# Regrouping the columns of a merged weight: 392 + 392 + a rest into 512 + 512 + a rest

## The reference, cut to what matters

```python
H = x @ W.T
xa = x @ A[adapter].T                       # rank 16
y = H + scal[adapter] * (xa @ Bm[adapter].T)
result = y @ base_w.T + base_b
logits = y @ router_w.T + router_b          # 8 experts
gate = top2(softmax(logits))                # normalised, spread over 8
mid = (y @ lora_A) * gate                   # 8 x 16 columns
x = x + result + 2.0 * (mid @ lora_B)
```

## Time and profile before

| | |
|---|---|
| median of 3 runs | 2394.57 us (2393.4 to 2395.55) |
| span of the profiled execution, first to last instruction | 2381.5 us |
| median less that span | 13.1 us |
| TensorE matmul, busy | 2354.5 us, 99% of the span |
| mean granted TensorE clock | 0.996 of full speed |
| weight stage, first matmul to last | 1781.8 to 1897.1 us |
| last stage, first matmul to end of the span | 1897.3 to 2381.5 us |

### The profile page before, as it was taken

One profiled execution on the slowest core, in us unless ns is written; L12 is line 12 of the kernel. 1 busy time (PEld: TensorE's weight loads), 2 busy tenths in 40 slices (PEclk: granted clock), 3 DMA queues, 4 the chain that ended last, 5 costly groups with the idle time before them and its releaser, 6 DMA issues.

```text
span 2381.5 us, 35318 instructions
## 1 busy us (share of the span) xinstructions
PE 2354.5 (99%) x12762; PEld 2074.8 (87%) x12762; DVE 1664.0 (70%) x2874; ACT 1369.5 (58%) x2256; POOL 1414.4 (59%) x1032
## 2 busy tenths in 40 slices
PE   8989999999999999999999999999999999999999
PEld 5778888888888888888888888888889999999999
DVE  6888888888888878888888788888862244444443
ACT  5767777777767767777777777777761211111110
POOL 4027888787778777777777777777710122222222
PEclk9999999999999999999999999999999999999999
DMA  9998999999998999989989989899876354444441
GB/s 343 385 328 283 285 291 272 288 282 287 278 298 279 284 282 280 281 277 287 282 274 288 284 276 282 275 290 280 274 196 132 87 140 130 130 130 130 128 121 60
DMA packets 250352, 582.33 MB, mean 245 GB/s; under 512 B 82745, under 2 KB 106682, under 8 KB 250178
## 3 DMA queue, kind: packets, MB, share of 16 engines
q1 hardware_dynamic: 183202, 401.18, 51.5%
q0 software_dynamic: 55584, 160.02, 26.0%
q10 hardware_dynamic: 11392, 18.88, 2.2%
HBM read 456.51 MB, written 123.45 MB: 244 GB/s over the span
## 4 chain that ended last, share of the span: by engine, by line
PE 93%; POOL 2%; DMA 2%; issue 1%; DVE 1%; ACT 0%; ACTq 0%; SPq 0%; DVEq 0%; POOLq 0%
PE ps L808 25%; PE ps L821 21%; PE ps L920 17%; PE ps L807 12%; PE ps L878 5%; PE ps L804 4%; PE ps L677 2%; PE ps L913 2%; PE ps L805 2%; POOL Xg L573 1%; PE ps L687 1%; PE ps L893 1%; DMA Xg<-yd,idx 1%; PE ps L700 1%; PE ps L699 0%
## 5 line engine op out<-in xcount | busy, mean ns | idle before, releaser
L808 PE MATMUL ps<-XX,HR 128*128 128x512 f32 x2688 | 961.0, 397 | 0.0
L573 POOL DMA_INDIRECT Xg<-yd,idx x504 | 663.4, 1316 | 160.5 <-issue 152.7
L807 PE MATMUL ps<-XX,LR 128*128 128x256 f32 x2688 | 751.2, 279 | 0.1
L1540 DVE TENSOR_TENSOR LR<-raw,HR 128x1536 fp32r<-128x1536 f32 x384 | 657.3, 1752 | 3.7 <-ACT HR L1075 3.6
L808 PEld LDWEIGHTS ps<-XX,HR 128*128 128x128 f32 x2688 | 505.9, 188 | 104.4
L1075 ACT ACTIVATE HR<-raw 128x1536 fp32r<-128x1536 f32 x384 | 556.5, 1478 | 11.8 <-DMA raw<-in_L_ffn_wd 8.9
L807 PEld LDWEIGHTS ps<-XX,LR 128*128 128x128 f32 x2688 | 508.3, 189 | 18.3 <-DVE LR L1540 0.7
L595 POOL DMA_INDIRECT accd<-ot,toki x128 | 253.0, 1977 | 149.9 <-ACT ot L1129 127.7
L920 PE MATMUL ps<-MH,xT 128*128 128x392 f32 x1536 | 335.8, 344 | 0.0
L821 PE MATMUL ps<-LR,hH 128*128 128x512 f32 x768 | 303.3, 395 | 0.0
L821 PE MATMUL ps<-HR,hH 128*128 128x512 f32 x768 | 299.8, 390 | 2.9 <-DVE LR L1540 2.2
(11 more groups left out here) (214 smaller groups left out, 3226.1 us busy)
## 6 DMA issues: line engine op xcount, KB each, us to landing
raw<-in_L_ffn_wd SPq DMA_DIRECT2D x128, 768.0 KB, 4.8
raw<-in_L_ffn_wg SPq DMA_DIRECT2D x126, 768.0 KB, 7.3
raw<-in_L_ffn_wu SPq DMA_DIRECT2D x126, 768.0 KB, 6.9
yd<-yrow ACTq DMA_DIRECT2D x32, 512.0 KB, 6.7
x<-accd SPq DMA_DIRECT2D x32, 512.0 KB, 5.2
out<-osb SPq DMA_DIRECT2D x31, 512.0 KB, 3.0
xt<-in_x SPq DMA_DIRECT2D x25, 512.0 KB, 8.2
accd<-xt SPq DMA_DIRECT2D x25, 512.0 KB, 6.6
```

Source lines behind the costliest of these rows:

```text
L573: eng.indirect_dma_start(Xg[:, c, q, :], None, yd4, bass.IndirectOffsetOnAxis(ap=idx4[:, e % 4, i:i + 1], axis=0))\
L807: eng.matmul(bank(out, 0, CAP), wl, xx[:, 0:CAP], start=False, stop=False)
L808: mm = eng.matmul(bank(out), wh, xx, start=False, stop=(k == 7))
L1540: eng.tensor_tensor(LR[:, (n + 2) % NHL, :], raw[:, n % NRAW, :], HR[:, (n + 2) % NHL, :].bitcast(F32), ALU.subtract).then_inc(s_L, 1)
```

## The change

The groups become 512, 512 and a rest of 136 columns, or 152 in `main` (with the 16 adapter columns). A triple in `main` still streams 1176 columns, and in the weight stage 1160. The low rank term covers 1024 columns and so needs two groups only: six matmuls of 512 in place of nine. The last block's steps stand at other counted places, and its final pieces are two in place of three.

```diff
--- before.py
+++ after.py
@@ -21,9 +21,11 @@
 NA = 8
 R = 16
 NX = D + NA + NA * R
-CG = [(0, 392), (392, 784), (784, NX)]
+CG = [(0, 512), (512, D), (D, NX)]
+GW = 512
+TW = NX - D + R
 MW = NX + 2 * R
-XA = [784, NX + R]
+XA = [D, NX + R]
 ORD = [8, 0, 1, 2, 3, 4, 5, 6, 7]
 UN = 1536
 NRAW = 4
@@ -502,12 +504,12 @@
                 if 6 <= t < NB + 1:
                     load_q(t - 1)
             t = NB - 1
-            for n, g in enumerate((2, 0, 1)):
-                a, z = CG[g][0], min(CG[g][1], D)
+            for n, g in enumerate((0, 1)):
+                a, z = CG[g]
                 eng.wait_ge(s_fin, 2 * t + 1 + n)
                 eng.dma_start(out_r[t * P:(t + 1) * P, a:z], osb[:, t % 3, a:z]).then_inc(d_o[t % 3], 16)
             for s in range(3):
-                eng.wait_ge(d_o[s], 16 * (len(range(s, NB, 3)) + (2 if s == t % 3 else 0)))
+                eng.wait_ge(d_o[s], 16 * (len(range(s, NB, 3)) + (1 if s == t % 3 else 0)))
 
         @block.gpsimd
         def _(eng):
@@ -900,24 +902,22 @@
                     eng.wait_ge(s_mtl, t)
                 eng.transpose(bank(7, 0, P), mg[:, :], ident[:, :]).then_inc(s_mt, 1)
 
-            def lora(t, groups=(0, 1, 2)):
+            def lora(t, groups=(0, 1)):
                 eng.wait_ge(s_mtl, t + 1)
                 if t == 0:
                     eng.wait_ge(s_lbl, 1)
-                b0, o = lbank(t), R * (1 - t % 2)
+                b0 = lbank(t)
                 for m, (X, Y) in enumerate([(mgH, lbH), (mgH, lbL), (mgL, lbH)]):
                     for g in groups:
                         a, z = CG[g]
-                        z = min(z, D)
-                        i = o if g == 2 else 0
-                        mm = eng.matmul(bank(b0 + g, i, i + z - a), X[:, :], Y[:, a:z], start=False, stop=(m == 2),
+                        mm = eng.matmul(bank(b0 + g), X[:, :], Y[:, a:z], start=False, stop=(m == 2),
                                         skip_group_check=True)
                 mm.then_inc(s_lo, 1)
 
             def main(t, k, m, n):
                 X = xtl(t) if m == 2 else xth(t)
-                a = (0, 392, XA[0] + R * (t % 2))[n]
-                return eng.matmul(bank(lbank(t) + n, 0, 392), X[:, k, :], (MH, ML, MH)[m][:, k, a:a + 392],
+                a, w = ((0, GW), (GW, GW), (XA[0] + R * (t % 2), TW))[n]
+                return eng.matmul(bank(lbank(t) + n, 0, w), X[:, k, :], (MH, ML, MH)[m][:, k, a:a + w],
                                   start=(k == 0 and m == 0), stop=(k == 7 and m == 2))
 
             for t in range(NB - 1):
@@ -950,26 +950,24 @@
             eng.wait_ge(s_xc, t + 1)
             for i in range(72):
                 mm = main(t, i % 24 // 3, i % 3, (2, 0, 1)[i // 24])
-                if i == 8:
+                if i == 16:
                     turn_a(t - 1)
-                if i == 17:
-                    adapter(t - 1)
                 if i == 23:
                     mm.then_inc(s_mm, 1)
-                if i == 35:
+                if i == 29:
+                    adapter(t - 1)
+                if i == 44:
                     turn_m(t - 1)
-                if i == 38:
+                if i == 47:
                     turn_a(t)
-                if i == 44:
+                if i == 52:
                     lora(t - 1)
                     adapter(t, (0, 2))
-                if i == 50:
+                if i == 56:
                     adapter(t, (1,))
-                if i == 62:
+                if i == 66:
                     turn_m(t)
-                if i == 68:
-                    lora(t, (2,))
-                    lora(t, (0,))
+            lora(t, (0,))
             lora(t, (1,))
 
         @block.scalar
@@ -1256,17 +1254,17 @@
                 eng.wait_ge(s_m, j + 1)
                 b0 = mbank(j)
                 if k == 8:
-                    eng.activation(MH[:, 7, 0:784].rearrange("p (g n) -> p g n", g=2), ps[:, b0:b0 + 2, 0:392], ACT.Copy,
+                    eng.activation(MH[:, 7, 0:D].rearrange("p (g n) -> p g n", g=2), ps[:, b0:b0 + 2, :], ACT.Copy,
                                    scale=scp[:, 0:1])
-                    eng.activation(MH[:, 7, 784:NX], bank(b0 + 2, 0, NX - 784), ACT.Copy, scale=scp[:, 0:1])\
+                    eng.activation(MH[:, 7, D:NX], bank(b0 + 2, 0, NX - D), ACT.Copy, scale=scp[:, 0:1])\
                        .then_inc(s_mh, 1)
                     return
                 if k == 6:
                     eng.wait_ge(d_at, 32)
                 if k == 7:
                     eng.wait_ge(d_m8, 48)
-                eng.activation(MH[:, k, 0:784].rearrange("p (g n) -> p g n", g=2), ps[:, b0:b0 + 2, 0:392], ACT.Copy)
-                eng.activation(MH[:, k, 784 + R:NX + R], bank(b0 + 2, 0, NX - 784), ACT.Copy).then_inc(s_mh, 1)
+                eng.activation(MH[:, k, 0:D].rearrange("p (g n) -> p g n", g=2), ps[:, b0:b0 + 2, :], ACT.Copy)
+                eng.activation(MH[:, k, D + R:NX + R], bank(b0 + 2, 0, NX - D), ACT.Copy).then_inc(s_mh, 1)
 
             def high_t():
                 for f in range(2):
@@ -1760,10 +1758,10 @@
                                                       MH[:, 7, a:z].bitcast(F32), ALU.mult, ALU.subtract)
                     mm.then_inc(s_ml, 1)
                     return
-                eng.tensor_tensor(ML[:, k, 0:784].rearrange("p (g n) -> p g n", g=2), ps[:, b0:b0 + 2, 0:392],
-                                  MH[:, k, 0:784].rearrange("p (g n) -> p g n", g=2).bitcast(F32), ALU.subtract)
-                eng.tensor_tensor(ML[:, k, 784 + R:NX + R], bank(b0 + 2, 0, NX - 784),
-                                  MH[:, k, 784 + R:NX + R].bitcast(F32), ALU.subtract).then_inc(s_ml, 1)
+                eng.tensor_tensor(ML[:, k, 0:D].rearrange("p (g n) -> p g n", g=2), ps[:, b0:b0 + 2, :],
+                                  MH[:, k, 0:D].rearrange("p (g n) -> p g n", g=2).bitcast(F32), ALU.subtract)
+                eng.tensor_tensor(ML[:, k, D + R:NX + R], bank(b0 + 2, 0, NX - D),
+                                  MH[:, k, D + R:NX + R].bitcast(F32), ALU.subtract).then_inc(s_ml, 1)
 
             def permute_a():
                 eng.wait_ge(d_ab, 32)
@@ -1812,7 +1810,7 @@
                     eng.wait_ge(s_xz, 1)
                 else:
                     eng.wait_ge(s_xat, t)
-                b2, o = lbank(t) + 2, 0 if t % 2 == 0 else 392 - R
+                b2, o = lbank(t) + 2, 0 if t % 2 == 0 else TW - R
                 eng.tensor_copy(xas[:, 0:3 * R].rearrange("p (h r) -> p h r", h=3),
                                 bank(b2, o, o + R).unsqueeze(1).to_broadcast([P, 3, R])).then_inc(s_xa, 1)
 
@@ -1852,27 +1850,22 @@
                    .then_inc(s_mtl, 1)
 
             def final(t):
-                b0, s, o = lbank(t), t % 6, R * (1 - t % 2)
+                b0, s = lbank(t), t % 6
                 eng.wait_ge(s_lo, t + 1)
                 eng.wait_ge(s_pb, t + 1)
                 if t >= 3:
                     eng.wait_ge(d_o[t % 3], 16 * (t // 3))
-                eng.tensor_tensor(osb[:, t % 3, 0:784].rearrange("p (g n) -> p g n", g=2), ps[:, b0:b0 + 2, 0:392],
-                                  x1[:, s, 0:784].rearrange("p (g n) -> p g n", g=2), ALU.add).then_inc(s_fin, 1)
-                eng.tensor_tensor(osb[:, t % 3, 784:D], bank(b0 + 2, o, o + D - 784), x1[:, s, 784:D],
-                                  ALU.add).then_inc(s_fin, 1)
+                for g, (a, z) in enumerate(CG[:2]):
+                    eng.tensor_tensor(osb[:, t % 3, a:z], bank(b0 + g), x1[:, s, a:z], ALU.add).then_inc(s_fin, 1)
 
             def final_last():
                 t = NB - 1
-                b0, s, o = lbank(t), t % 6, R * (1 - t % 2)
+                b0, s = lbank(t), t % 6
                 eng.wait_ge(s_pb, t + 1)
                 eng.wait_ge(d_o[t % 3], 16 * (t // 3))
-                for n, g in enumerate((2, 0, 1)):
-                    a, z = CG[g]
-                    z = min(z, D)
-                    i = o if g == 2 else 0
+                for n, (a, z) in enumerate(CG[:2]):
                     eng.wait_ge(s_lo, t + 1 + n)
-                    eng.tensor_tensor(osb[:, t % 3, a:z], bank(b0 + g, i, i + z - a), x1[:, s, a:z], ALU.add)\
+                    eng.tensor_tensor(osb[:, t % 3, a:z], bank(b0 + n), x1[:, s, a:z], ALU.add)\
                        .then_inc(s_fin, 1)
 
             turn_r(1)

```

## The result

The changed kernel takes 2435.1 us (median, 2431.7 to 2437.1) beside 2394.0 us for the kernel before on the same chip: the ratio is 1.0174, with a 95% interval of 1.0162 to 1.0186. That is +41 us. Forecast were 2429 us and a range of 2418 to 2440.

The account below looks back on a forecast made before the run. TensorE's start-to-start matmul rate was taken to bound both stages, short rests being limited by weight loads. Main +25.3, weight stage +8.6, adapter +1.6, lora -1.0, start -0.4, end +0.2 sum to +34.3 us: 2429 us, range 2418 to 2440.

Parts of the forecast that it names:

- The price of a rest: Weight and last stage: a matmul of 152 or 136 columns costs one weight load, 110 ns, ends 107 and 112.
- The plain float32 row with 64 columns: Layer 0 of the kernel before: 64-column matmuls with full 128x128 loads start 110 ns apart, taken as the load's floor.
- The slope of the load's duration: Loads of 64 and 128 weight columns last 135 and 188 ns, so 128 columns occupy the loader for 106 or 107.
- The sign to look for: Profile after: 107 to 112 ns from a rest to the next matmul; near 70 the forecast is wrong, nothing is lost.
- The price of a 512: Weight and last stage: a 512-column matmul was taken as 230 ns, ends 229 and 234.
- `lora`: Low rank term, last stage: nine matmuls of 1.41 us become six of 1.38 us, 32 times: -1.0 us.
- `adapter`: Last stage: its three matmuls go from 0.52 us to 0.57, 32 times: +1.6 us.
- Start and end of the last stage: Start: the 0.6 us wait shrinks, -0.4 us (0 to -0.6); end: wider last add and store, +0.2 us (+0.1 to +0.4).
- 13.1 us around the span: Whole kernel before: median run time exceeds the profiled 2381.5 us span by 13.1 us, which the change leaves alone.
- Hidden behind more than one matmul: Rival, both stages: the loader runs two ahead, a rest costs only streaming, 70 or 63 ns; 2387 us, chance 0.06.
- half hidden: Rival, both stages: the load is partly covered, a rest costs about 90 ns; 2409 us, chance 0.05.
- No overlap at all: Rival, both stages: a load does not overlap a short matmul, a rest costs 177 ns; 2495 us, chance 0.03.

Follow-up runs that it names:

- the split: The changed kernel with main's 152-column rest in the last stage issued as two matmuls of 76 columns: 2523.9 us, ratio 1.0536 to the kernel before.

## Why the prediction was right, point by point

- **What bounds it.** Right: both stages are TensorE's, at full clock, before and after, and matmul distances are the currency. No other engine came to bound the last stage.
- **The price of a rest.** Right in mechanism and size: 110 ns taken, with 107 and 112 as ends; 108 measured, by load distances and by the split. The plain float32 row with 64 columns carries over to float32r. The slope of the load's duration gave the right number too, but with some luck: a load for a transpose, also of 128 columns, lasts only 0.14 us, so columns alone do not set the duration. And the forecast charged every rest, where the two a block ahead of the transposes cost 70 ns.
- **The sign to look for.** Wrong: I wrote that the distance "from a rest of 136 or 152 columns to the next" would be 107 to 112, and that near 70 "nothing is lost". It is 70 and 63, and the loss is there all the same, some 40 ns in the 512 behind, which takes 0.27 to 0.28 us to the next start in place of 0.23. A row of the kernel before warned of it, one line on from the earlier trace rows in the timeline of its matmuls:

```profile
68.87 1.08 PE L677 MATMUL ps<-xkB,wall 128*128 128x512 f32 x2
```

  The load of this matmul starts at 68.81, only 0.06 us ahead of it, where loads take 0.11. So a start in this record is not the arrival of the weights. The distance of loads, or the sum over a whole triple, is the proof.
- **The price of a 512.** The mis-sized term: 230 taken, some 234 measured in the last stage (a triple is 108 + 232 + 236 = 576, where 570 was taken), and not only around a rest: `lora`'s six take 1.40 / 6 = 233 each (next point). `main` grows by 24 x (577 - 537) ns a block, less 2 x 38 for the rests ahead of the transposes: 0.88 us, so 32 x 0.88 = 28 us for 25.3 forecast. The weight stage comes to 9.9 for 8.6.
- **`lora`.** Mis-sized, small: the forecast was 1.38 us a block, a gain of 1.0 us. The chain has 1.44, but 0.04 of it is the stall behind `main`'s last rest, booked on `lora`'s first 512 (and `main`'s piece behind `lora`, with no rest ahead of it, is 5.14 where the other is 5.19). Where a 512 stands ahead of it, in the run with the rest in the middle, `lora` takes 1.40:

```profile
2168.37 1.40 PE ps L914 x6
```

  So it gains 0.01 us a block, 0.3 us in all. Three matmuls fewer gain next to nothing, since the columns stay.
- **`adapter`** 0.57 us as forecast, against 0.52 in the row. It takes over one stall and hands on another.
- **Start and end of the last stage.** The 0.6 us wait is gone, the far end of the forecast's 0 to 0.6: from 1921.83 us on the chain has 81 matmuls without a break. All of the last stage is +29.5, where its terms (25.3 + 1.6 - 1.0 - 0.4 + 0.2) made 25.7.
- **The sum.** +34.3 forecast, +39.4 in the traces' two stages, +41 in the timings. The frame of "13.1 us around the span" was a misreading that did no harm, because it was left alone on both sides. Had I compared spans, it would have made the change look 54 us long.
- **The rivals.** "Hidden behind more than one matmul" and "half hidden" are out: in the last stage of the changed kernel no load starts sooner than the matmul ahead of its own (1 to 4 ns behind that start, or some 40 where a stall is booked), and a short matmul leaves it uncovered even where three loads would fit in the triple. "No overlap at all" (177 ns) is out too. Of the Trainium skill's "TensorE: Matmul & The Clock Gate", section "Back-to-back issue gap", neither the formula for a lone matmul (66 ns at 152 columns, no load in it) nor the pair price of about 81 ns at 128 columns holds for float32r here: the measured pair is 108.

## What to carry to other kernels

Where each matmul brings its own 128x128 float32r load, its price is the larger of 108 ns and 0.45 ns a column, so a rest under about 240 columns is paid as 240: keep every group above that before filling banks. Equal groups are one way, and 512, 424 and 240 did as well in `main`. Fewer matmuls with the same columns gain next to nothing once all are above that width. And judge such a change by load distances or whole groups, for the record books the stall under the innocent matmul behind.

No regrouping that was tried beat the kernel before: with 1176, 1160 and 1024 columns in three groups of 392, 392 and a rest of 392, 376 or 240, none of these matmuls is under the corner, and the nearest of the alternatives was 0.4% slower.

## What was not expected of the hardware

- A matmul's recorded start can precede by some 40 ns the point from which its distances say that it runs (2031.13 against 2031.17), with the duration stretched by as much: 0.44 us for such a 512 in place of 0.39.
- A 512 costs 229 ns among its like in the experts and some 234 in the last stage, beside a rest or not, at the same clock. Why is open.
- A rest of 152 columns costs 108 ns ahead of a float32r matmul and 70 ahead of a transpose.
- The granted clock fell to 1.2 GHz for 10 us in the run with the rest cut in two, though TensorE was busy throughout with 76-column matmuls. In the changed kernel's last block, with 24 of 152 columns in a row, it stayed at 2.4 GHz.
- The part ahead of the experts was 10 to 12 us shorter in one trace of ten than in the nine others, one of them of the same kernel.
